# Half of the spread gates loaded from DRAM, expert units in pairs, and the last FFN's weights divided during the second layer, in a two-layer vision tower

## The reference

```python
h = tok(x)
h = ln(h + attn0(h))    # low-rank q, k, v; 12 heads
h = ln(h + ffn0(h))     # 64 slots, each with its own 192x768 and 768x192 matrix, soft routing
h = ln(h + attn1(h))    # two softmax maps, out1 - exp(lambda) * out2
h = ln(h + ffn1(h))     # routed experts, below
```

```python
z = einsum('nd,sdr->nsr', xf, P)
scores = einsum('nsr,smr->nsm', z, C)
topv, topi = top_k(scores, 4)
w = softmax(topv)
h = gelu(einsum('nsr,nskrh->nskh', z, W1[topi]) + b1[topi])
comb = einsum('nskr,nsk->nsr', einsum('nskh,nskhr->nskr', h, W2[topi]) + b2[topi], w)
out = gelu(comb.reshape(n, 128) @ G1 + g1b) @ G2 + g2b
```

## Time and profile before

| | us |
|---|---|
| median of 3 runs | 959.13 |
| the runs | 952.45, 961.68, 959.13 |
| the profiled execution's own time | 950.38 |
| its span | 948.3 |
| first FFN, weights streaming (from the windows) | about 204 to 388 |
| second attention | about 398 to 597 |
| routing of three tiles | about 597 to 634 |
| experts, first to last product on DVE | 634.5 to 921.9 |
| tail | to 948.3 |

### The profile page before, as it was taken

One profiled execution on the slowest core, in us unless ns is written; L12 is line 12 of the kernel. 1 busy time (PEld: TensorE's weight loads), 2 busy tenths in 40 slices (PEclk: granted clock), 3 DMA queues, 4 the chain that ended last, 5 costly groups with the idle time before them and its releaser, 6 DMA issues.

```text
span 948.3 us, 17188 instructions
## 1 busy us (share of the span) xinstructions
PE 768.0 (81%) x6440; PEld 425.4 (45%) x6440; DVE 539.9 (57%) x1499; ACT 381.0 (40%) x786; POOL 149.0 (16%) x187
## 2 busy tenths in 40 slices
PE   5989997797877785558889897448888988899992
PEld 3667766653333333236666666223333333333331
DVE  5666567401110111158685867737877686878776
ACT  0432424132111110023443343236777676768760
POOL 0030321322221000040111010322202122200002
PEclk9977779579798686669998999758888998999997
DMA  7611000049999999690000000570002000200001
GB/s 300 255 39 38 4 1 2 1 169 423 425 424 414 410 422 363 108 110 4 2 2 0 0 1 2 158 97 1 1 1 51 1 1 1 51 5 2 1 1 39
DMA packets 25017, 102.66 MB, mean 108 GB/s; under 512 B 3551, under 2 KB 14755, under 8 KB 20723
## 3 DMA queue, kind: packets, MB, share of 16 engines
q1 hardware_dynamic: 23894, 98.36, 31.0%
q0 software_dynamic: 1056, 3.44, 0.9%
HBM read 93.08 MB, written 5.07 MB: 103 GB/s over the span
## 4 chain that ended last, share of the span: by engine, by line
PE 58%; DVE 17%; DMA 13%; issue 4%; ACT 2%; POOL 2%; SPq 1%; DVEq 0%; POOLq 0%; ACTq 0%
DMA stream<-in_fc_dram 13%; PE P L1670 9%; PE P L1638 8%; PE P L1648 8%; PE P L367 6%; PE P L795 3%; PE P L439 3%; PE P L410 3%; PE P L1132 2%; PE P L423 2%; DVE work L603 2%; DVE work L504 1%; DVE early L483 1%; PE P L1663 1%; PE P L764 1%
## 5 line engine op out<-in xcount | busy, mean ns | idle before, releaser
L1895 DVE TENSOR_TENSOR work<-work,P 128x384 f32<-128x384 f32 (+1 forms) x384 | 197.5, 560 | 73.5 <-PE P L1648 60.5
L1777 ACT ACTIVATE work<-P 128x384 f32<-128x384 f32 (+1 forms) x384 | 177.7, 500 | 71.5 <-PE P L1638 63.5
L1638 PE MATMUL P<-stream 99*128 99x384 bf16 (+1 forms) x384 | 136.1, 355 | 20.4 <-ACT work L1777 13.4
L1648 PE MATMUL P<-early,middle 96*128 96x384 bf16 (+1 forms) x384 | 135.5, 353 | 11.0 <-DVE work L1895 5.8
L1638 PEld LDWEIGHTS P<-stream 99*128 99x128 bf16 x384 | 38.9, 102 | 119.6 <-ACT work L1777 67.6
L1670 PE MATMUL P<-work 128*32 128x384 f32 (+1 forms) x768 | 89.7, 539 | 0.0
L822 ACT ACTIVATE work<-P 128x768 f32<-128x768 f32 x16 | 13.0, 811 | 157.2 <-PE P L777 157.2
L514 ACT ACTIVATE work<-work 101x444 f32<-101x444 f32 x48 | 28.1, 585 | 103.9 <-DVE work L509 103.9
L837 DVE COPY work<-P 128x768 f32<-128x768 f32 x16 | 15.3, 958 | 94.8 <-PE P L785 94.8
L1648 PEld LDWEIGHTS P<-early,middle 96*128 96x128 bf16 x384 | 39.2, 102 | 50.0 <-DVE work L1895 27.7
L608 POOL TENSOR_SCALAR work<-work 101x4 f32<-101x4 f32 x12 | 2.8, 229 | 345.1 <-DVE work L598 345.1
(11 more groups left out here) (254 smaller groups left out, 1261.6 us busy)
## 6 DMA issues: line engine op xcount, KB each, us to landing
stream<-in_fc_dram SPq DMA_DIRECT2D x16, 2304.0 KB
stream<-in_fc_dram SPq DMA_DIRECT2D x16, 1536.0 KB, 18.3
stream<-in_fc_dram SPq DMA_DIRECT2D x16, 768.0 KB, 19.7
early<-in_patches_dram SPq DMA_DIRECT2D x4, 888.0 KB, 5.1
stream<-w_dram SPq DMA_DIRECT2D x6, 512.0 KB
early<-stream SPq DMA_DIRECT2D x24, 96.0 KB, 3.1
work<-in_w_dram SPq DMA_DIRECT2D x1, 2048.0 KB, 7.7
stream<-z_dram SPq DMA_DIRECT2D x6, 297.0 KB, 10.2
```

The lines of the kernel that those rows point to most:

```text
L1638: pe.matmul(P[:, n % 3, 0:WIDE[c]], w1s[:, seg, (hh * (CH // 2) + i) * 128:(hh * (CH // 2) + i + 1) * 128], zs[:, seg, part_of(c)], start= ...
L1648: pe.matmul(P[:, 3 + n % 3, 0:WIDE[c]], gate_sel[:, i, :], ws[:, 2 * (4 * sq + j) + hh, part_of(c)], start=True, stop=True).then_inc(s_bc, 1)
L1777: act.activation(act_out[:, n % 4, 0:cols], P[:, n % 3, 0:cols], ACT.Gelu_apprx_tanh).then_inc(s_ua, 1)
L1895: dve.tensor_tensor(gated[:, n % 8, 0:cols], act_out[:, n % 4, 0:cols], P[:, 3 + n % 3, 0:cols], ALU.mult).then_inc(s_ug, 1)
```

## The change

- **Gates.** Of each four units, two (`j` 0, 1) get their gates as before by PE, in one pair. For the other two the gate rows stay f32 (`gate_rest`), SP stores them to DRAM (`store_gates`), and for each group of four units one transfer (`load_spread`) reads four DRAM rows, each 32 times, into 128 partitions: 3072 or 3328 bytes to a partition. There are 96 of these loads and four buffers for them. Stagings into `ws` stay 12 to a chunk, with half the bytes.
- **Pairs.** ACT and DVE take two units in an instruction (128x768 or 128x832). Hidden rows have two pairs of banks (0 to 3), spread gates one pair (4, 5). The product with PE's gates reads PSUM, that with the loaded gates only SBUF.
- **Second bias.** One f32 and six bf16 matmuls in place of twelve.
- **Dividing weights.** SP loads `w1` and `b1` after the first FFN; POOL divides them in the first three steps of the second attention, SP stores and stacks them then. The row of ones is set in the fourth step.
- **Last group.** `first(15)` goes ahead of `second(14)`.

```diff
-        gate_parts = tenant(stream, 128, 0, [PARTS, 4, TZ], bf16)
+        gate_parts = tenant(stream, 128, 0, [PARTS, 2, TZ], bf16)
+        gate_rest = tenant(stream, 128, PARTS * TZ, [2, TZ])
+        spare = PARTS * TZ + 2 * TZ
...
-        act_out = w([128, 4, 416])
+        act_out = [w([128, 2, 416]), w([128, 2, 416])]
...
+        spread_at = (2 * TP, 2 * TP + 832, 6 * TP, 6 * TP + 832)
...
+        gate_dram = [dram(f"gate_dram{c}", [2, SM, 2, cols], f32) for c, cols in enumerate((384, 384, 416))]
...
+            sp.wait_ge(s_fo, GROUPS)
+            for n in range(4):
+                sp.dma_start(split_in[:, n, :], io["w1"][:, n * 512:(n + 1) * 512]).then_inc(s_split_in, 16)
+            sp.dma_start(split_in[:, 4, 0:128], io["b1"]).then_inc(s_split_in, 16)
+        def split_sync(sp):
+            def store(n, dst, cols):
+                sp.wait_ge(s_split, 4 * n + 4)
+                sp.dma_start(dst, split_out[:, :, 0:cols]).then_inc(s_split_out, 16)
+            for n in range(4):
+                store(n, w1_dram.rearrange("n p c -> p n c")[:, :, n * 512:(n + 1) * 512], 512)
+                if n == 0:
+                    sp.dma_start(split_in[:, 0, :], io["b2"]).then_inc(s_split_in, 16)
+                    sp.dma_start(b2_rest[:, :, :],
+                                 io["b2"].rearrange("p (a b r) -> p b a r", b=2, r=128)[:, 1]).then_inc(s_late2, 16)
+                elif n < 3:
+                    sp.dma_start(split_in[0:PARTS * 32, n, :], io["gate_sel"][:, n - 1]).then_inc(s_split_in, 16)
+            store(4, b1_dram.rearrange("n p c -> p n c"), 128)
...
+            first(GROUPS // 2 - 1, 1)
             second(GROUPS // 2 - 1, 0)
-            first(GROUPS // 2 - 1, 1)
...
+        def split(pool, base, src, out):
+            pool.tensor_copy(out[:, 0, :], src).then_inc(s_split, 1)
+            pool.wait_ge(s_split, base + 1)
+            pool.tensor_tensor(src, src, out[:, 0, :], ALU.subtract).then_inc(s_split, 1)
+            pool.wait_ge(s_split, base + 2)
+            pool.tensor_copy(out[:, 1, :], src).then_inc(s_split, 1)
+            pool.wait_ge(s_split, base + 3)
+            pool.tensor_tensor(out[:, 2, :], src, out[:, 1, :], ALU.subtract).then_inc(s_split, 1)
+        def split_w1(pool, n):
             pool.wait_ge(s_split_in, 16 * 5)
-            parts(128, 128, split_out[:, :, 0:128], 16)
-            pool.dma_start(b1_dram.rearrange("n p c -> p n c"), split_out[:, :, 0:128]).then_inc(s_split_out, 16)
-            pool.wait_ge(s_split_out, 16 * 5)
-            pool.dma_start(split_in[:, :], io["b2"]).then_inc(s_split_in, 16)
-            pool.wait_ge(s_split_in, 16 * 6)
-            parts(128, 512, b2s[:, :, :, :].rearrange("p n s r -> p n (s r)"), 20)
+            if n:
+                pool.wait_ge(s_split_out, 16 * n)
+            cols = 512 if n < 4 else 128
+            split(pool, 4 * n, split_in[:, n, 0:cols], split_out[:, :, 0:cols])
...
+                if it < 2:
+                    split_w1(pool, 2 * it)
+                    split_w1(pool, 2 * it + 1)
+                elif it == 2:
+                    split_w1(pool, 4)
+                    split_b2(pool)
+                elif it == 3:
+                    pool.wait_ge(s_split_out, 16 * 5)
+                    pool.wait_ge(s_h3, it)
+                    pool.memset(zs[6 * SR:ZR, :, :], 1.0).then_inc(s_set, 1)
+                    pool.wait_ge(s_set, 1)
+                if not last:
...
-            pool.wait_ge(s_fo, GROUPS)
-            pool.wait_ge(L0["rstd"], QUADS + 1)
-            pool.memset(zs[6 * SR:ZR, :, :], 1.0).then_inc(s_set, 1)
-            pool.wait_ge(s_set, 1)
-            steps(pool, step)
+            for it in range(QUADS):
+                step(it, it == 0, it + 1 == QUADS)
...
+            def store_gates(first, last):
+                sp.wait_ge(s_gr, last + 1)
+                c = first // 3 if first < 9 else 2
+                here = slice(128 * first, min(128 * (last + 1), FROM[c] + WIDE[c]))
+                for k in range(2):
+                    dst = gate_dram[c].rearrange("q r k t -> k r q t")[k]
+                    sp.dma_start(dst[:, :, here.start - FROM[c]:here.stop - FROM[c]],
+                                 gate_rest[SM * k:SM * (k + 1), :, here]).then_inc(s_gd, 16)
+            def stage_chunk(n):
+                tiles = -(-(FROM[n] + WIDE[n]) // 128)
                 if n:
                     sp.wait_ge(s_ws, n * STACKED)
-                tiles = -(-(FROM[n] + WIDE[n]) // 128)
                 for part, made in enumerate((s_g0, s_g1, s_g2)):
                     sp.wait_ge(made, tiles)
-                    stage_gates(sp, n, part)
-        def stage_gates(eng, n, part):
-            for q in range(4):
-                dst = ws[32 * part:32 * (part + 1), :, part_of(n)]
-                eng.dma_start(dst.rearrange("p (s q) t -> p q s t", q=4)[:, q],
-                              gate_parts[32 * q:32 * (q + 1), part, :, part_of(n)]).then_inc(s_ws, 16)
+                    stage_gates(n, part)
+            def stage_gates(n, part):
+                for q in range(4):
+                    dst = ws[32 * part:32 * (part + 1), :, part_of(n)]
+                    sp.dma_start(dst.rearrange("p (s q) t -> p q s t", q=4)[:, q, 0::2],
+                                 gate_parts[32 * q:32 * (q + 1), part, :, part_of(n)]).then_inc(s_ws, 16)
+            def load_spread(g):
+                c, sq, hh, i = GROUP[g]
+                if g % NG == 0:
+                    sp.wait_ge(s_gd, 32 * (1, 4, 8)[c])
+                if g >= RING:
+                    sp.wait_ge(s_ug, 2 * (g - RING) + 2)
+                row = 32 * hh + 4 * i
+                src = gate_dram[c][sq, row:row + 4].rearrange("r k t -> r (k t)")
+                sp.dma_start(spread_gates(g).rearrange("p k t -> p (k t)"), spread(src, 1, 32)).then_inc(s_sg[g % RING], 16)
+            store_gates(0, 2)
+            stage_chunk(0)
+            for g in range(3 * NG):
+                for t in range(FIRST, TT):
+                    if g == (BEGINS[t] + 16) // 2 + RING + 1:
+                        store_gates(t, t)
+                if g in (NG, 2 * NG):
+                    stage_chunk(g // NG)
+                load_spread(g)
...
+            def hidden_pair(g, x):
+                c, sq, hh, i = GROUP[g]
+                if g:
+                    pe.wait_ge(s_ua, 2 * (g - 1) + x + 1)
+                for j in (2 * x, 2 * x + 1):
+                    seg = 4 * sq + j
+                    mm = pe.matmul(P[:, j, 0:WIDE[c]], w1s[:, seg, (hh * (CH // 2) + i) * 128:(hh * (CH // 2) + i + 1) * 128],
+                                   zs[:, seg, part_of(c)], start=True, stop=True)
+                mm.then_inc(s_u1, 1)
...
+            def gate_pair(g):
+                c, sq, hh, i = GROUP[g]
+                if g % NG == 0:
                     pe.wait_ge(s_ws, (c + 1) * STACKED)
-                if n >= 3:
-                    pe.wait_ge(s_ug, n - 2)
-                pe.matmul(P[:, 3 + n % 3, 0:WIDE[c]], gate_sel[:, i, :], ws[:, 2 * (4 * sq + j) + hh, part_of(c)],
-                          start=True, stop=True).then_inc(s_bc, 1)
+                if g:
+                    pe.wait_ge(s_ug, 2 * (g - 1) + 1)
+                for j in range(2):
+                    mm = pe.matmul(P[:, 4 + j, 0:WIDE[c]], gate_sel[:, i, :], ws[:, 2 * (4 * sq + j) + hh, part_of(c)],
+                                   start=True, stop=True)
+                mm.then_inc(s_bc, 1)
...
+                pe.matmul(P[:, 6 + sq, 0:WIDE[c]], b2_rest[:, sq, :], gate_rest[:, sq, part_of(c)],
+                          start=True, stop=False, skip_group_check=True)
+                for g, b in PRODUCTS:
+                    pe.matmul(P[:, 6 + sq, 0:WIDE[c]], b2s[:, b, sq, :], gate_parts[:, g, sq, part_of(c)],
+                              start=False, stop=False, skip_group_check=True)
...
+            hidden_pair(0, 0)
+            hidden_pair(0, 1)
+            gate_pair(0)
+            for g in range(3 * NG):
+                if g + 1 < 3 * NG:
+                    hidden_pair(g + 1, 0)
+                if g:
+                    expert_out(g - 1)
+                if g + 1 < 3 * NG:
+                    hidden_pair(g + 1, 1)
+                    gate_pair(g + 1)
+                for x in range(2):
+                    t = beside(2 * g + x, 0)
                     if t:
                         scores(t)
-                    t = beside(k, 21)
+                    t = beside(2 * g + x, 12)
                     if t:
                         turn_gates(t)
-                if n >= 4:
-                    c, sq, hh, i, j = UNITS[n - 4]
-                    if (hh, i) == (0, 0):
-                        last_bias(c, sq)
-                    for k in range(n - 4, n):
-                        expert_out(k)
-                if n > NU and n % NU == 12:
-                    out_hidden(n // NU - 1)
+                if g > NG and g % NG == 3:
```

(65 more changed lines are left out.)

180 lines of the change are left out of this document (62 added, 118 removed).

## The result

The changed kernel takes 1051.3 us (median of four runs, 1046.7 to 1052.36) against 955.8 before (951.75 to 961.68): ratio 1.0985, 95% interval 1.0908 to 1.1061. It is slower by about 95 us; the forecast was 1036. The profiled run has a span of 1050.6 us and a time of 1052.36.

What follows compares the result with a forecast made beforehand. PE set the experts' pace, DVE close behind; changed, the loads would. Last load lands at 1015.3, plus 27.0 and 0.5 is 1042.8, less 18 is 1025; with 2.1 outside, 1027, and 8.8 to the median, 1036. Range 888 to 1085.

Steps and rivals of the forecast that it cites:

- The decisive step: Experts' stage: four engines carry each load at 104 GB/s, 3.78 us; above 3.0 us a load the change loses.
- Rival A: Experts' stage: loads use all 16 engines, 0.94 us each, DVE is the bound; median 895, 870 to 920; chance 0.31.
- Size of a load: Experts' stage: a load costs 3.78 us, 4.10 at 416 columns; 96 end to end come to 369.3 us.
- The start: Start of the experts' stage: first load lands at 638, less 18 us for the early edits.
- the row of ones: Second layer's first scaling: moving the memset away takes 6.5 us off.
- Order and dividing: First FFN: reordering its last group gains 5 us; moving the division and its transfers later gains 7 us.
- The last weights don't bind: End of the first FFN: the last weights land by about 378, so PE does not wait for them.
- together 18 off: Ahead of the experts: 7 + 6.5 + 5, less 0.5, taken whole off the span.
- The tail: From the last product to the end: 27.0 us as before, plus 0.5 for the pair.
- the last step: Whole kernel: adds 8.8 us because the earlier profiled run was that far under its median, giving 1036.
- DVE waiting for the DMA some 1.5 us a group: Experts' stage, expected sign: DVE's second product waits some 1.5 us a group for its load.
- PE's clock dropping: Experts' stage, expected sign: PE's clock drops; no size given.

Runs made afterwards that it cites:

- E3: Changed kernel with each load of four rows issued as two transfers of two rows: 1434.5 us.
- E1: Changed kernel with each gate row stored four times in DRAM, so a load's source begins with 16: 910.9 us, ratio to before 0.9504.
- E11: Changed kernel, gates stored once, each group's load as four one-row transfers that begin with 32 repeats; median of four runs 903.4 us, ratio to before 0.9482.
- E6: Changed kernel with each gate row stored twice, so a load's source begins with 8; median of four runs 906.5 us, ratio to before 0.9447.
- E9: Kernel before the change with only the last expert group reordered, `first(15)` ahead of `second(14)`: 956.7 us, one run.
- E5: Kernel before the change with only the early edits: division in the second layer's steps, memset in the last quad, last group reordered: 933.1 us, ratio 0.9777.
- E10: Kernel before the change with only the memset of the row of ones moved into the last quad's step: 945.1 us, one run.
- E2: Changed kernel with each gate row stored twice, the same kernel as E6: 894.6 us, one run.
- E4: Changed kernel with loads only for the first four groups of the stage and of the third chunk, 88 loads left out: 895.1 us.
- E7: Changed kernel where, past the first four loads of the stage and of the third chunk, each load brings only one of its two gates: 910.2 us.
- E8: Same change as E11, four one-row transfers a group that begin with 32 repeats, against the changed kernel: 900.9 us, one run.

## Why the prediction was right, and where it was off

**The decisive step held.** "A source that begins with four keeps a load on four engines", 104 GB/s, above the break-even of 3.0 us: every experiment on the load agrees. Four engines give 1051, two 1434, eight and sixteen 895 to 911. The Trainium skill, "DMA: Bandwidth & Descriptors", section "Why a DMA increments its semaphore by 16 and not by 1", gives this rule; the runs agree, with sides that differ (source 4, 8 and 16 against 128 partitions, 2 against 64), which the trace of before couldn't show. It also states that on this kind of queue the lowest-numbered engines are taken; the halves of E3 sharing two engines fit that, but no run here shows the numbers.

**Rival A's place.** With 16 engines the forecast put 895, 870 to 920. E1 and E11, with 16, give 911 and 903, and E6, with eight, 906. So the rival's premise alone was false. What the pairs are worth it had somewhat too high: 240 us for a stage of 288, where the runs show 248 to 251 for one of 287. The group takes 2.0 us, as worked out.

**Size of a load.** 3.78 and 4.10 us forecast. In undisturbed stretches the loaded products stand 3.9 and 4.2 us apart: 393,216 bytes in 3.9 us is 101 GB/s, not 104. With the stagings and stores between, the last loaded product (1019.49) starts 391.8 us after the first (627.66), forecast 377.3: 14.5 us of the miss. By the spacing of the products about 10 of these are the rate, the rest the transfers between.

**The start.** The first loaded product was to come at 638 - 18 = 620 and came at 627.7: 7.7. The early edits gave 11.7 at the first product in place of 18. Of their parts only the row of ones can be priced alone: 6.5 forecast, 9.38 - 3.05 = 6.3 measured. Order and dividing, 5 and 7 forecast, gave 8.9 together at the end of the last `second`. How that divides is open: from the stage's first matmul to there it is 191.3 to 195.4 us in the three traces without the dividing, 183.1 to 185.2 in the ten with both. "The last weights don't bind" failed: PE waited for them in E9 (3.37 us) and in the changed kernel (2.87).

At the end of the scaling 14.7 us of the 18 are there. The step "together 18 off" missed that it isn't carried through: at the last kept output 11.2 are left. The 3.5 go ahead of the first kept output, for from first to last of them it is 122.4 us before and 122.7 in the changed kernel. There the granted clock was 0.89 before and 0.85 in the changed kernel, for the same 554 matmuls; E5 and E10, also at 0.85, lose 3.7 and 4.7 of their gain by the last kept output, E10 without any division step, so the division isn't the cause. Whether a shorter scaling brings the lower clock with it is not shown. The 7.7 are in any case no more than chance can give: with one and the same program up to there, the traces have the experts' first product between 614.4 and 630.6.

**The tail.** From the last loaded product to the end: 31.1 us, forecast 27.5: 3.6. The prediction put no term for the clock here. Behind the last loaded product it was 0.52 in the changed kernel and 0.73 in E11. Windows from the last loaded product to the end, in the changed kernel and in E11:

```profile
1019.50:1050.60 31.10, 15.10 (x72) 6.72 (x72) 15.62 (x57) 1.11 (x2) 5.06 (x8) 0.52 0.13 30
```
```profile
866.70:894.30 27.60, 8.99 (x76) 4.36 (x76) 15.52 (x58) 1.11 (x2) 5.07 (x8) 0.73 0.15 34
```

E3, which waits for its loads as well, has 31.1 us here too; E1, E2, E4, E6, E7, E8 and E11 have 27.6 to 27.8.

**The median.** 7.7 + 14.5 + 3.6 = 25.8 us above the forecast span of 1024.8, and the span is 1050.6. Of that 8.8 us were taken back by the last step, adding the distance of the profiled run to the median; this time the profiled run lay 1 us above its median. So 1051 against 1036 is the balance of two misses of opposite sign, and that it came within 15 us is in part luck.

**What should have been seen** was: a DMA share near 0.25 at 104 GB/s (0.257, 101), groups 3.8 apart (3.9), no POOL transfers. Not seen: "DVE waiting for the DMA some 1.5 us a group" stands under ACT's name, at 2.1 to 2.3 us. "PE's clock dropping" did not happen in the stage, 0.97 against 0.92 before, with PE idle a quarter of the time; it came in the tail, 0.52. Under two engines it dropped in the stage, to 0.67.

**Better than both.** Two or four stored copies or four transfers a group turn the change into a gain of about 5% (0.9447 to 0.9504): 903 to 911 us. About 24 of these 45 to 53 us are the early edits' (E5).

## What to carry to other kernels

Before a load that repeats few rows over many partitions is trusted with a place on the path, read its access pattern from the front: a leading dimension of four meant four of 16 engines here, and two narrow transfers shared the same two. Put the repeats in front, or store copies so that the leading dimension is a multiple of 16. The count of packets under 512 bytes tells the engines of a transfer after the run. A gain of a few us counts only when several traces show it alike: the same kernel began its last stage 16 us apart in two of them. And a wait on several semaphores is checked by the time at which the named engine produced the very buffer read.

## What the runs showed that was not expected

Spread over more engines, each engine carries less. By GB/s over DMA share the stretch from 700 to 800 us comes to 161 / 0.52 = 310 with eight engines a load and 165 / 0.62 = 266 with sixteen, against 106 / 0.29 = 366 with four. Windows of that stretch in E6, then in E1, and last one of E11's third chunk, in which only loads were issued:

```profile
700.00:800.00 100.00, 88.89 (x574) 31.14 (x572) 84.00 (x183) 76.30 (x108) 26.98 (x32) 0.98 0.52 161
```
```profile
700.00:800.00 100.00, 87.06 (x561) 30.55 (x560) 83.08 (x178) 74.21 (x105) 25.54 (x31) 0.97 0.62 165
```
```profile
800.00:860.00 60.00, 59.88 (x404) 20.43 (x406) 53.14 (x55) 44.81 (x58) 0.00 (x0) 0.99 0.66 196
```

So the 0.94 us a load that I had from the weights' 420 GB/s is too low; by 266 it is nearer 1.5. It is hidden here either way. The stagings and stores are in the shares of the first two windows. They aren't the whole of it, for E11's window, without any, comes to 196 / 0.66 = 297, where four engines alone come to 101 / 0.257 = 393 between 900 and 1000 us. Nor are the small packets the likely cause: E11 has 64 of them a group to E1's 16, and a rate no lower. The cause stays open.
